# A graph network of four layers on one core: edge sources, destinations and weights stored as one table of rows

## The chip, the core and the metric

The kernel runs on one core of a Trainium2 chip. A core has five engines, each with its own instruction queue: TensorE (PE: matmuls, with PEld for the weight loads), VectorE (DVE), ScalarE (ACT), GpSimd (POOL) and SyncE (SP, which only issues DMAs). They share an on-chip memory of 128 partitions and 16 DMA engines that move data to and from device memory. The metric is the device time of one execution in microseconds (us). 0.2% of it, 13.2 us, is about what a measurement can tell from no change.

## The reference

There are 6250 nodes of 128 features and 100000 edges; `dst` is sorted, `src` is random. Each layer normalizes, applies a relu, passes messages along the edges, sums them by destination and adds the result to `x`:

```
edge_index = stack([src, dst])
x = x + L0(relu(layernorm(x)), edge_index, edge_weight)       # gather * weight, segment_sum, @W0, batch norm, relu
x = x + L1(relu(layernorm(x)), edge_index)                    # relu(h@Wmsg+b)[src], segment_sum, update, + h
x = x + L2(relu(layernorm(x)), edge_index, edge_attr_64)      # silu/sigmoid message from [h[src], h[dst], e]
x = x + L3(relu(layernorm(x)), node_vec1, src, dst, edge_attr_4, edge_attr_8)
```

In layer 0 `edge_index[0]` (src) is the row that is summed into and `edge_index[1]` (dst) the one gathered from, with the factor `edge_weight`.

## The kernel before

**Work items.** The sorted edges are cut into 782 rows of 128 (`ROWS`; 781 whole ones and one of 32 edges, filled up by 96). Nodes are in 49 blocks of 128, one partition for each node of a block. An item is one row of edges seen from one node block; there are 832 (`ITEMS`), and the setup finds for each its block and its row of edges. The item tables `src_it`, `rel_it` and `w_it` hold, for each item, the 128 sources, the 128 destinations relative to the block and the 128 weights, one item to a column.

**Setup, up to the first barrier.** ACT copies `src`, `dst` and `edge_weight` to device-memory arrays `e_src`, `e_dst`, `e_w` (L966), padded to a whole number of rows. SP loads `dst` for DVE (L349), then `x` (L354, L355), 34 weights and biases (L357), then stores what a possible sort would need: `blk_i`, `blk_f`, `bin_next` (L360 to L363). POOL writes the filling of the last row (L558, six DMAs), clears a buffer of zeros (L561), drains, stores it to four arrays `sums0` to `sums3` (L565), which layer 0 adds its messages to, and waits for the plan and for SP's three stores (`blocks_out`, L616). `dst` is sorted here, so the branch L573 to L612 is not run. Then POOL issues 21 indirect gathers (L625 to L627, for each of seven chunks of 128 items one from each of the three arrays): partition p gets the 512 bytes of its item's row. DVE meanwhile makes the plan (L1166 to L1221), then scales weights (L1256 to L1267), waits at L1273 until all 21 gathers have landed (`meta_rows`), turns what came into floats (L1275 to L1279), and PE transposes it into the item tables (L695, copies L1285). At the end of it each engine drains its queue and waits until all five have done so (`barrier`, L237): the first barrier, L628 on POOL, L1291 on DVE. Behind it DVE starts the layer norm (L1296); POOL waits for the zeroing (L632) and goes to a second barrier, which ends `node_tables(0)`.

**Layer 0.** For each item SP loads the row of sources to all partitions (`src_b`, L392), DVE, PE and ACT make a 128x128 tile of messages, and POOL adds it to one of the four `sums` by an indirect DMA (L642), 832 times. Layers 1 to 3 gather node rows with 2496 indirect DMAs (L670). The order on every engine is that of the program text; DMAs of different engines share the 16 DMA engines.

Of the kernel before, what the change touches and what calls it, by code (L numbers as in the profile page):

```python
# [18 lines left out]
ALU = mybir.AluOpType  # L19
ACT = mybir.ActivationFunctionType  # L20
F32 = mybir.dt.float32
I32 = mybir.dt.int32
# [3 lines left out]
P = 128  # L26
N = 6250
E = 100000
# [3 lines left out]
ROWS = (E + P - 1) // P  # L32
EPAD = ROWS * P
# [4 lines left out]
META = CHUNKS * P  # L38
# [19 lines left out]
def gnn_layers(nc, x, src, dst, edge_attr_4, edge_attr_64, edge_attr_8, edge_weight,  # L58
               W0, gamma, beta, Wmsg, bmsg, Wupd, bupd, w1, b1, w2, b2, wg, bg, wu, bu,
               wl1s, wl1v, fc1, fc2, wl2s, wl2v, out):  # L60
    with ExitStack() as ctx:
# [8 lines left out]
        def dram(name, shape, dt=F32):  # L70
            return nc.dram_tensor(name, shape, dt, kind="Internal").ap()


        e_src, e_dst, e_w = dram("e_src", [EPAD, 1], I32), dram("e_dst", [EPAD, 1], I32), dram("e_w", [EPAD, 1])
        e_a4, e_a8, e_a64 = dram("e_a4", [2 * EPAD, 4]), dram("e_a8", [2 * EPAD, 8]), dram("e_a64", [2 * EPAD, 64])
        e_pre = dram("e_pre", [QUADS + 4, P, 4, 256])
        blk_f, blk_i, bin_next = dram("blk_f", [E, 1]), dram("blk_i", [E, 1], I32), dram("bin_next", [64, 1])
# [206 lines left out]
        def landed(each, ring, q, k, lag):  # L284
# [2 lines left out]
                return each * ((q - lag) // ring + 1)  # L287
            return (q - k) * (each // ring) + each * ((k - lag) // ring + 1)

        def batches(layer):  # L290

            n = NODE_BATCH[layer]
            return [(i, b, min(n, NBT - b)) for i, b in enumerate(range(0, NBT, n))]
# [53 lines left out]
        def _(sp):  # L347
# [33 lines left out]
            def load_attributes(layer):  # L381

                ph = EDGE[layer]
                freed = ph["dup_done"]
                regs = [sp.alloc_register(f"row{layer}_{k}") for k in range(RING)]

                def top(turn):
                    sp.load(regs, row_row[0:1, bass.ds(turn + LEAD, RING)])

                def load(k, turn):  # L390
                    r = sp.snap(regs[k], min_val=0, max_val=ROWS - 1)
                    sp.dma_start(src_b[:, k, :], e_src[bass.ds(r * P, P), :].rearrange("e o -> (o e)").partition_broadcast(P)  # L392
                                 ).then_inc(attr_in[k], 16)

                half = sp.value_load(copy_to[0:1, 0:1], min_val=0, max_val=EPAD)

                def copy(at, n):
                    for to, of in ((e_a64, edge_attr_64), (e_a8, edge_attr_8), (e_a4, edge_attr_4)):
                        even = lambda a: a.rearrange("e k -> (e k)").rearrange("(q c) -> q c", q=16 if n == FIRST else P)
                        sp.dma_start(even(to[bass.ds(half + at, n), :]),  # L400
                                     even(of[bass.ds(at, n) if not isinstance(at, int) else slice(at, at + n), :])).then_inc(a64_copied, 16)

                top(0)
                for k in range(RING):
                    load(k, 0)
                copy(0, FIRST)
                with sp.Fori(RING, ITEMS - RING + 1, RING) as turn:
                    copy((turn - RING) * (PIECE // RING) + FIRST, PIECE)
                    top(turn)
                    for k in range(RING):  # L410

                        held(sp, freed, turn + (k - RING + 1))
                        load(k, turn)
# [107 lines left out]
        def _(pool):  # L521
# [31 lines left out]
            pool.wait_ge(tail_ready, 1)  # L553

            def tails():
                for to, of in ((e_src, s_i[0:TN, 0:1]), (e_dst, s_i[0:TN, 1:2]), (e_w, s_f[0:TN, 0:1]),
                               (e_a4, s_64[0:TN, 0:4]), (e_a8, s_64[0:TN, 0:8]), (e_a64, s_64[0:TN, 0:64])):
                    pool.dma_start(to[T0:EPAD, :], of).then_inc(tails_in, 16)  # L558
            tails()
            zeros = big[:, 9000:9000 + (NBT + 1) * P]  # L560
            g.memset(zeros, 0.0)  # L561
            pool.drain().then_inc(tail_ready, 1)
            pool.wait_ge(tail_ready, 2)
            for k in range(COPIES):
                pool.dma_start(sums[k].rearrange("(p b) d -> p (b d)", p=P), zeros).then_inc(scattered[k], 16)  # L565
            pool.wait_ge(tails_in, 6 * 16)


# [4 lines left out]
            with pool.Else():  # L573


                pool.wait_ge(blocks_out, 48)
                pool.wait_ge(small_copied, 48)

                def tile(t, e0, n, first):
                    sl = slice(e0, e0 + n) if isinstance(e0, int) else bass.ds(e0, n)  # L580
                    if not first:

                        held(pool, sort_pos, t)
                        for k in range(2):
                            held(pool, sort_out[k], t * 48)
                        held(pool, sort_bin, t * 16)
                    pool.dma_start(s_bb[:, 0:n], blk_f[sl, :].rearrange("e o -> o e").partition_broadcast(P)).then_inc(sort_in[0], 16)
                    for q, (to, of) in enumerate(((s_f[0:n, 1:2], blk_f[sl, :]), (s_i[0:n, 2:3], blk_i[sl, :]),
                                   (s_i[0:n, 0:1], src[sl].rearrange("(e o) -> e o", o=1)),
                                   (s_i[0:n, 1:2], dst[sl].rearrange("(e o) -> e o", o=1)),  # L590
                                   (s_f[0:n, 0:1], edge_weight[sl].rearrange("(e o) -> e o", o=1)),
                                   (a12[0:n, 0, 0:4], edge_attr_4[sl, :]), (a12[0:n, 1, 0:8], edge_attr_8[sl, :]),
                                   (s_64[0:n, :], edge_attr_64[sl, :]))):
                        pool.dma_start(to, of).then_inc(sort_in[q // 4], 16)
                    held(pool, sort_in[0], t * 80 + 80)
                    held(pool, sort_in[1], t * 64 + 64)
                    pool.indirect_dma_start(s_f[0:n, 2:3], None, bin_next,
                                            bass.IndirectOffsetOnAxis(ap=s_i[0:n, 2:3], axis=0)).then_inc(sort_base, 16)

                    held(pool, sort_rank, t + 1)  # L600
                    pool.dma_start(bin_next, s_f[0:64, 5:6]).then_inc(sort_bin, 16)
                    at = bass.IndirectOffsetOnAxis(ap=s_i[0:n, 3:4], axis=0)
                    for q, (to, of) in enumerate(((e_src, s_i[0:n, 0:1]), (e_dst, s_i[0:n, 1:2]), (e_w, s_f[0:n, 0:1]),
                                                  (e_a4, a12[0:n, 0, 0:4]), (e_a8, a12[0:n, 1, 0:8]), (e_a64, s_64[0:n, :]))):
                        pool.indirect_dma_start(to, at, of, None).then_inc(sort_out[q // 3], 16)
                full = E // P
                tile(0, 0, P, True)
                with pool.Fori(1, full) as t:
                    tile(t, t * P, P, False)
                tile(full, full * P, E - full * P, False)  # L610
                for k in range(2):
                    pool.wait_ge(sort_out[k], (full + 1) * 48)  # L612

            pool.nop()

            pool.wait_ge(blocks_out, 48)  # L616
            pool.wait_ge(small_copied, 48)


            rows128 = lambda a: a.rearrange("(r e) o -> r (e o)", e=P)  # L620
            m_i = big[:, 0:2 * META].bitcast(I32)
            m_w = big[:, 2 * META:3 * META]
            for c in range(CHUNKS):
                at = bass.IndirectOffsetOnAxis(ap=it_ai[:, c:c + 1], axis=0)
                pool.indirect_dma_start(m_i[:, c * P:(c + 1) * P], None, rows128(e_src), at).then_inc(meta_rows, 16)  # L625
                pool.indirect_dma_start(m_i[:, META + c * P:META + (c + 1) * P], None, rows128(e_dst), at).then_inc(meta_rows, 16)
                pool.indirect_dma_start(m_w[:, c * P:(c + 1) * P], None, rows128(e_w), at).then_inc(meta_rows, 16)  # L627
            barrier(pool)  # L628


# [330 lines left out]
        @block.scalar  # L961
        def _(act):
            a = nc.scalar
            flat = lambda a, c: a.rearrange("(q c) o -> q (c o)", c=c)
            for to, of in ((e_src, src), (e_dst, dst), (e_w, edge_weight)):
                act.dma_start(flat(to[0:E, :], EC), of.rearrange("(q c) -> q c", c=EC)).then_inc(small_copied, 16)  # L966

            act.wait_ge(const_ready, 3)
            act.wait_ge(blocks_ready, 1)
# [182 lines left out]
        def _(dve):  # L1152
# [114 lines left out]
            v.tensor_scalar(Wl2[32:64, 1, 0:32], Wl2[32:64, 1, 0:32], float(3 ** -0.5), None, ALU.mult)  # L1267


            m_i = big[:, 0:2 * META].bitcast(I32)  # L1270
            m_w = big[:, 2 * META:3 * META]
            m_f = big[:, 3 * META:6 * META]
            dve.wait_ge(meta_rows, 16 * 3 * CHUNKS)  # L1273
            link(v.tensor_scalar(it_off[:], it_b[:], float(P), None, ALU.mult))
            v.tensor_copy(m_f[:, 0:META], m_i[:, 0:META])  # L1275
            v.tensor_copy(m_f[:, 2 * META:3 * META], m_w)
            for c in range(CHUNKS):
                lo = META + c * P
                last = v.tensor_scalar(m_f[:, lo:lo + P], m_i[:, lo:lo + P], it_off[:, c:c + 1], None, ALU.subtract)  # L1279
            dve.drain().then_inc(meta_rel, 1)  # L1280
            for q in range(3 * CHUNKS):
                dve.wait_ge(meta_T, q + 2)
# [413 lines left out]
```

## Time and profile before

| | us |
|---|---|
| three runs | 6579.94, 6580.35, 6586.99 (median 6580.35) |
| profiled execution | 6581.73 |
| its span | 6580.1 |
| setup, to the first instruction behind the first barrier | 119.08 |
| layer 0's first indirect sum | 170.22 |
| POOL busy in the whole span | 3778.7 (57%) |
| PE, DVE, ACT busy | 4451.8, 3511.6, 1918.0 |

A profile shows one execution. In a timeline a row is an instruction or several like ones on one engine, with its start, its length, and in brackets how long the engine had been idle and what released it. SPq and ACTq are the queues that issue DMAs: the length is that of the issue, not of the transfer. In a table of windows stand the busy time of each engine in a stretch, the granted clock of TensorE as a share of its full clock, the mean busy share of the 16 DMA engines, and the GB/s that they moved.

### The profile page before, as it was taken

The numbers are of one execution on the slowest core, as the hardware profiler recorded it, in microseconds if no ns is written. First come the engines' busy times: TensorE is split into PE (matmuls) and PEld (weight loads), VectorE is DVE, ScalarE is ACT, GpSimd is POOL, SyncE is SP. The second block draws the span as 40 slices with busy tenths as digits, with TensorE's granted clock in tenths as the row PEclk, the third lists the DMA queues.
The fourth block names the chain that finished last, engine by engine and source line by source line (L and its number), as shares of the span: only waits on it lengthen the run. The fifth ranks groups of instructions, "written<-read, shape, count | busy, mean of one in ns | idle before, by whom it ended". The sixth has DMA issues, their size and how long they took to land. (4 is left out here: it accounts for less than half of the span.)

```text
span 6580.1 us, 113728 instructions
## 1 busy us (share of the span) xinstructions
PE 4451.8 (68%) x21582; PEld 3403.9 (52%) x21583; DVE 3511.6 (53%) x11197; ACT 1918.0 (29%) x5540; POOL 3778.7 (57%) x3395
## 2 busy tenths in 40 slices
PE   1888888888345555656777777777765666666667
PEld 1666666666234444444565656565554444444445
DVE  5655555555443232332655655555565555656555
ACT  2322222222122222222322222222243333333333
POOL 2888888888356666665255555555515454555443
PEclk9555555555577777777889888888886667777667
DMA  4666665666434454444244444444412222222222
GB/s 135 101 90 93 89 93 92 90 92 90 95 112 152 155 156 152 154 154 148 97 138 139 140 136 138 136 141 134 137 55 39 37 38 37 37 38 37 37 38 44
DMA packets 822279, 660.17 MB, mean 100 GB/s; under 512 B 444329, under 2 KB 711251, under 8 KB 820826
## 3 DMA queue, kind: packets, MB, share of 16 engines
q0 software_dynamic: 214432, 287.62, 22.0%
q1 hardware_dynamic: 607674, 370.53, 20.3%
q10 hardware_dynamic: 96, 1.20, 0.1%
q8 instruction: 24, 0.39, 0.0%
q14 instruction: 53, 0.43, 0.0%
HBM read 464.78 MB, written 225.68 MB: 105 GB/s over the span
## 5 line engine op out<-in xcount | busy, mean ns | idle before, releaser
L670 POOL DMA_INDIRECT G<-table,src_it x2496 | 2417.5, 969 | 2121.0 <-issue 651.1
L1388 DVE TENSOR_TENSOR big<-psum,big 128x129 f32 (+2 forms) x2496 | 823.6, 330 | 1225.0 <-remote 596.0
L642 POOL DMA_INDIRECT sums<-work,idx x832 | 1284.1, 1543 | 318.4 <-issue 179.2
L800 PE MATMUL psum<-work 128*128 128x128 f32 x1664 | 631.0, 482 | 192.8 <-DVE work L1435 115.0
L887 PE MATMUL psum<-big,oh 128*128 128x256 f32 x1664 | 643.7, 554 | 8.2 <-ACT big L1091 3.5
L1037 ACT ACTIVATE work<-psum,work 128x128 f32<-128x128 f32 x832 | 305.4, 367 | 1066.4 <-PE psum L792 667.4
L800 PEld LDWEIGHTS psum<-work 128*128 128x128 f32 x1664 | 414.0, 308 | 384.0 <-DVE work L1435 243.5
L747 PE MATMUL psum<-We,work 64*128 64x256 f32 x1664 | 347.0, 552 | 375.1 <-ACT work L1016 295.0
L1375 DVE TENSOR_TENSOR oh<-iota,rel_it 128x512 f32<-128x512 f32 x625 | 438.5, 702 | 298.5 <-remote 143.5
L792 PE MATMUL psum<-big,work 128*128 x1664 | 586.1, 455 | 0.0
L887 PEld LDWEIGHTS psum<-big,oh 128*128 128x128 f32 x1664 | 444.7, 280 | 134.0 <-issue 41.8
L1427 DVE TENSOR_SCALAR work<-G,src_it 128x128 f32<-128x128 int32 x832 | 268.3, 322 | 392.1 <-PE psum L800 308.6
L878 PE MATMUL psum<-ident,work 128*32 128x128 f32 x208 | 69.0, 332 | 557.3 <-DMA work<-e_a 431.6
L747 PEld LDWEIGHTS psum<-We,work 64*128 64x128 f32 x1664 | 212.9, 268 | 435.8 <-issue 352.5
L792 PEld LDWEIGHTS psum<-big,work 128*128 128x128 f32 x1664 | 414.2, 309 | 26.3 <-issue 8.7
L784 PE MATMUL psum<-ident,oh 128*128 128x128 f32 x832 | 366.3, 440 | 83.8 <-issue 46.9
L1050 ACT ACTIVATE work<-psum 128x512 f32<-128x512 f32 x208 | 124.2, 597 | 969.4 <-remote 512.2
L820 PE MATMUL psum<-big,work 128*128 x2496 | 377.0, 300 | 31.2 <-ACT work L1063 28.0
L1009 ACT ACTIVATE work<-psum 128x256 f32<-128x256 f32 x208 | 79.7, 383 | 970.0 <-remote 480.6
L1075 ACT ACTIVATE work<-psum 32x128 f32<-32x128 f32 x208 | 55.4, 266 | 1019.5 <-PE psum L878 676.4
L1493 DVE TENSOR_TENSOR work<-psum,work 128x512 f32<-128x512 f32 x416 | 267.2, 684 | 157.8 <-remote 72.9
L1435 DVE COPY work<-psum 128x128 f32<-128x128 f32 x832 | 242.5, 291 | 179.8 <-DMA sums<-work,idx 172.5
(230 smaller groups left out, 7709.9 us busy)
## 6 DMA issues: line engine op xcount, KB each, us to landing
e_pre<-work SPq DMA_DIRECT2D x208, 512.0 KB
work<-e_pre SPq DMA_DIRECT2D x208, 512.0 KB
G<-e_src SPq DMA_DIRECT2D x832, 64.0 KB
G<-table,src_it POOLq DMA_INDIRECT x2496
work<-e_a SPq DMA_DIRECT2D x832, 32.0 KB
e_a<-in_edge_attr_dram SPq DMA_DIRECT2D x51, 488.0 KB
sums<-work,idx POOLq DMA_INDIRECT x832
work<-e_a SPq DMA_DIRECT2D x832, 4.0 KB
```

The lines of the kernel that those rows point to most:

```text
L642: pool.indirect_dma_start(sums[k % COPIES], bass.IndirectOffsetOnAxis(ap=idx[:, k:k + 1], axis=0), z_out[:, k, :], None, compute_op=ALU.ad ...
L670: pool.indirect_dma_start(G[:, k, 0:wid], None, tab, bass.IndirectOffsetOnAxis(ap=src_it[:, n:n + 1], axis=0)).then_inc(quad_in[k // 4], 16)
L747: mm = t.matmul(bank[5 + j % 2][:, j // 2 * 256:j // 2 * 256 + 256], eT1[h:h + 64, (k - 1) % 2, j // 2, :], We2[h:h + 64, :], start=True, ...
L784: t.transpose(bank[s % 2][:, 0:P], oh[:, s, :], ident[:]).then_inc(ph["t_done"], 1)
L792: t.matmul(bank[2 + s % 2][:, 0:P], ohT[:, s % 4, :], at(Tz, b), start=True, stop=True).then_inc(ph["row_done"], 1)
L800: t.matmul(bank[4 + s % 2][:, 0:P], same[:, s % 4, :], scaled[:, s % 4, :], start=True, stop=True).then_inc(ph["sum_done"], 1)
L820: mm = t.matmul(bank[1 + j // 2][:, j % 2 * 256:j % 2 * 256 + 256], ohT2[:, j, :], Qp[:, bass.ds(b, 1), piece * 256:(piece + 1) * 256].rea ...
L887: mm = t.matmul(bank[4 + k % 2 * 2 + j // 2][:, j % 2 * 256:j % 2 * 256 + 256], oh[:, k % 4 * 4 + j, :], msg3[:, k % 4, j, :], start=True, ...
L1037: a.activation(scaled[:, s % 4, :], bank[2 + s % 2][:, 0:P], ACT.Copy, scale=w_it[:, bass.ds(n - 4, 1)]).then_inc(ph["w_done"], 1)
L1375: v.tensor_tensor(oh[:, k % 4 * 4:k % 4 * 4 + 4, :], iota[:].unsqueeze(1).broadcast_to([P, 4, P]), rel_it[:, bass.ds(q * 4, 4)].unsqueeze( ...
L1388: v.tensor_tensor(to, ps, to, ALU.add).then_inc(EDGE[layer]["acc_done"], 1)
L1427: v.tensor_scalar(same[:, s % 4, :], src_b[:, s, :], src_it[:, bass.ds(n - 1, 1)], None, ALU.is_equal).then_inc(ph["same_ready"], 1)
```

## The change

The three arrays become one table `e_meta` of 782 rows with 3 x 128 elements, so 1536 bytes: sources, destinations, weights of a row of edges side by side.

- ACT copies each input into its third of the rows (`meta_parts`: 781 pieces of 512 bytes and one short piece), six DMAs in place of three.
- POOL's three small tail stores go to the last row of `e_meta`.
- POOL zeroes `sums0` and `sums1` where it zeroed all four, and `sums2` and `sums3` behind the gathers, before the first barrier.
- The gathers are 7 of 1536 bytes a partition in place of 21 of 512 bytes. DVE reads the three parts with a stride, and waits for 7.
- Layer 0's loads of sources read the first third of a row of `e_meta`.
- If `dst` were not sorted, the sorted arrays would be copied into `e_meta` too; this isn't run.

```diff
@@ -71,7 +71,8 @@
             return nc.dram_tensor(name, shape, dt, kind="Internal").ap()
 
 
-        e_src, e_dst, e_w = dram("e_src", [EPAD, 1], I32), dram("e_dst", [EPAD, 1], I32), dram("e_w", [EPAD, 1])
+        e_src, e_dst, e_w = dram("e_src", [E, 1], I32), dram("e_dst", [E, 1], I32), dram("e_w", [E, 1])
+        e_meta = dram("e_meta", [ROWS, 3, P], I32)
         e_a4, e_a8, e_a64 = dram("e_a4", [2 * EPAD, 4]), dram("e_a8", [2 * EPAD, 8]), dram("e_a64", [2 * EPAD, 64])
         e_pre = dram("e_pre", [QUADS + 4, P, 4, 256])
         blk_f, blk_i, bin_next = dram("blk_f", [E, 1]), dram("blk_i", [E, 1], I32), dram("bin_next", [64, 1])
@@ -287,6 +288,14 @@
                 return each * ((q - lag) // ring + 1)
             return (q - k) * (each // ring) + each * ((k - lag) // ring + 1)
 
+        def meta_parts(src, dst, weight):
+
+            whole = ROWS - 1
+            for q, of in enumerate((src, dst, weight)):
+                to = e_meta.bitcast(F32) if q == 2 else e_meta
+                yield to[0:whole, q, :], of[0:whole * P].rearrange("(r e) -> r e", e=P)
+                yield to[whole:ROWS, q, 0:E - whole * P], of[whole * P:E].rearrange("(r e) -> r e", r=1)
+
         def batches(layer):
 
             n = NODE_BATCH[layer]
@@ -389,7 +398,7 @@
 
                 def load(k, turn):
                     r = sp.snap(regs[k], min_val=0, max_val=ROWS - 1)
-                    sp.dma_start(src_b[:, k, :], e_src[bass.ds(r * P, P), :].rearrange("e o -> (o e)").partition_broadcast(P)
+                    sp.dma_start(src_b[:, k, :], e_meta[bass.ds(r, 1), 0, :].rearrange("o e -> (o e)").partition_broadcast(P)
                                  ).then_inc(attr_in[k], 16)
 
                 half = sp.value_load(copy_to[0:1, 0:1], min_val=0, max_val=EPAD)
@@ -553,16 +562,21 @@
             pool.wait_ge(tail_ready, 1)
 
             def tails():
-                for to, of in ((e_src, s_i[0:TN, 0:1]), (e_dst, s_i[0:TN, 1:2]), (e_w, s_f[0:TN, 0:1]),
-                               (e_a4, s_64[0:TN, 0:4]), (e_a8, s_64[0:TN, 0:8]), (e_a64, s_64[0:TN, 0:64])):
+                for q, of in enumerate((s_i[0:TN, 0:1], s_i[0:TN, 1:2], s_f[0:TN, 0:1])):
+                    to = e_meta.bitcast(F32) if q == 2 else e_meta
+                    pool.dma_start(to[ROWS - 1, q, P - TN:P].rearrange("(e o) -> e o", o=1), of).then_inc(tails_in, 16)
+                for to, of in ((e_a4, s_64[0:TN, 0:4]), (e_a8, s_64[0:TN, 0:8]), (e_a64, s_64[0:TN, 0:64])):
                     pool.dma_start(to[T0:EPAD, :], of).then_inc(tails_in, 16)
             tails()
             zeros = big[:, 9000:9000 + (NBT + 1) * P]
             g.memset(zeros, 0.0)
             pool.drain().then_inc(tail_ready, 1)
             pool.wait_ge(tail_ready, 2)
-            for k in range(COPIES):
+
+            def zero(k):
                 pool.dma_start(sums[k].rearrange("(p b) d -> p (b d)", p=P), zeros).then_inc(scattered[k], 16)
+            for k in range(2):
+                zero(k)
             pool.wait_ge(tails_in, 6 * 16)
 
 
@@ -574,7 +588,7 @@
 
 
                 pool.wait_ge(blocks_out, 48)
-                pool.wait_ge(small_copied, 48)
+                pool.wait_ge(small_copied, 96)
 
                 def tile(t, e0, n, first):
                     sl = slice(e0, e0 + n) if isinstance(e0, int) else bass.ds(e0, n)
@@ -610,21 +624,24 @@
                 tile(full, full * P, E - full * P, False)
                 for k in range(2):
                     pool.wait_ge(sort_out[k], (full + 1) * 48)
+                column = lambda a: a.rearrange("e o -> (e o)")
+                for to, of in meta_parts(column(e_src), column(e_dst), column(e_w)):
+                    pool.dma_start(to, of).then_inc(sort_in[0], 16)
+                pool.wait_ge(sort_in[0], (full + 1) * 80 + 96)
 
             pool.nop()
 
             pool.wait_ge(blocks_out, 48)
-            pool.wait_ge(small_copied, 48)
-
-
-            rows128 = lambda a: a.rearrange("(r e) o -> r (e o)", e=P)
-            m_i = big[:, 0:2 * META].bitcast(I32)
-            m_w = big[:, 2 * META:3 * META]
+            pool.wait_ge(small_copied, 96)
+
+
+            meta_rows_of = e_meta.rearrange("r t e -> r (t e)")
+            m_all = big[:, 0:3 * META].bitcast(I32)
             for c in range(CHUNKS):
-                at = bass.IndirectOffsetOnAxis(ap=it_ai[:, c:c + 1], axis=0)
-                pool.indirect_dma_start(m_i[:, c * P:(c + 1) * P], None, rows128(e_src), at).then_inc(meta_rows, 16)
-                pool.indirect_dma_start(m_i[:, META + c * P:META + (c + 1) * P], None, rows128(e_dst), at).then_inc(meta_rows, 16)
-                pool.indirect_dma_start(m_w[:, c * P:(c + 1) * P], None, rows128(e_w), at).then_inc(meta_rows, 16)
+                at_rows = bass.IndirectOffsetOnAxis(ap=it_ai[:, c:c + 1], axis=0)
+                pool.indirect_dma_start(m_all[:, c * 3 * P:(c + 1) * 3 * P], None, meta_rows_of, at_rows).then_inc(meta_rows, 16)
+            for k in range(2, COPIES):
+                zero(k)
             barrier(pool)
 
 
@@ -961,9 +978,8 @@
         @block.scalar
         def _(act):
             a = nc.scalar
-            flat = lambda a, c: a.rearrange("(q c) o -> q (c o)", c=c)
-            for to, of in ((e_src, src), (e_dst, dst), (e_w, edge_weight)):
-                act.dma_start(flat(to[0:E, :], EC), of.rearrange("(q c) -> q c", c=EC)).then_inc(small_copied, 16)
+            for to, of in meta_parts(src, dst, edge_weight):
+                act.dma_start(to, of).then_inc(small_copied, 16)
 
             act.wait_ge(const_ready, 3)
             act.wait_ge(blocks_ready, 1)
@@ -1267,16 +1283,17 @@
             v.tensor_scalar(Wl2[32:64, 1, 0:32], Wl2[32:64, 1, 0:32], float(3 ** -0.5), None, ALU.mult)
 
 
-            m_i = big[:, 0:2 * META].bitcast(I32)
-            m_w = big[:, 2 * META:3 * META]
+            m_i = big[:, 0:3 * META].bitcast(I32).rearrange("p (c t e) -> p c t e", t=3, e=P)
+            m_w = big[:, 0:3 * META].rearrange("p (c t e) -> p c t e", t=3, e=P)
+            chunked = lambda a: a.rearrange("p (c e) -> p c e", e=P)
             m_f = big[:, 3 * META:6 * META]
-            dve.wait_ge(meta_rows, 16 * 3 * CHUNKS)
+            dve.wait_ge(meta_rows, 16 * CHUNKS)
             link(v.tensor_scalar(it_off[:], it_b[:], float(P), None, ALU.mult))
-            v.tensor_copy(m_f[:, 0:META], m_i[:, 0:META])
-            v.tensor_copy(m_f[:, 2 * META:3 * META], m_w)
+            v.tensor_copy(chunked(m_f[:, 0:META]), m_i[:, :, 0, :])
+            v.tensor_copy(chunked(m_f[:, 2 * META:3 * META]), m_w[:, :, 2, :])
             for c in range(CHUNKS):
                 lo = META + c * P
-                last = v.tensor_scalar(m_f[:, lo:lo + P], m_i[:, lo:lo + P], it_off[:, c:c + 1], None, ALU.subtract)
+                last = v.tensor_scalar(m_f[:, lo:lo + P], m_i[:, c, 1, :], it_off[:, c:c + 1], None, ALU.subtract)
             dve.drain().then_inc(meta_rel, 1)
             for q in range(3 * CHUNKS):
                 dve.wait_ge(meta_T, q + 2)
```

On POOL, from the end of the unused sort branch to layer 0. `big` is the on-chip buffer that the gathered rows go to. Before:

```order
L625 DMA big<-e_src,big 128x128 [waits small_copied,blocks_out]
L626 DMA big<-e_dst,big 128x128
L627 DMA big<-e_w,big 128x128
...
L627 DMA big<-e_w,big 128x128
L644 UNCONDITIONAL_BRANCH [waits scattered2,scattered1,scattered3,scattered0,phase_end]
L644 ISA
```

The same place in the changed program (L577 is the zeroing):

```order
L642 DMA big<-e_meta,big 128x384 [waits small_copied,blocks_out]
L642 DMA big<-e_meta,big 128x384 x6
L577 DMA sums<-big 128x6528 x2
L661 UNCONDITIONAL_BRANCH [waits scattered2,scattered1,scattered3,scattered0,phase_end]
L661 ISA
```

21 gathers have become 7, and two zeroings stand between them and the barriers. Earlier on POOL, from the last tail stores on, before:

```order
L558 DMA e_a<-big 96x8
L558 DMA e_a<-big 96x64
L561 MEMSET big 128x6528
L565 DMA sums<-big 128x6528 [waits tail_ready]
L565 DMA sums<-big 128x6528 x3
L570 TENSOR_LOAD big [waits plan_ready,tails_in]
```

and now:

```order
L569 DMA e_a<-big 96x8
L569 DMA e_a<-big 96x64
L572 MEMSET big 128x6528
L577 DMA sums<-big 128x6528 [waits tail_ready]
L577 DMA sums<-big 128x6528
L584 TENSOR_LOAD big [waits plan_ready,tails_in]
```

Two zeroings are left there of four. The start of ACT's queue, before:

```order
L966 DMA e_src<-in_src_dram 16x6250
L966 DMA e_dst<-in_dst_dram 16x6250
L966 DMA e_w<-in_edge_weight_dram 16x6250
L974 ACT_TABLE_LOAD [waits blocks_ready]
L974 ACTIVATE big<-big 125x800 [waits const_ready]
```

and now:

```order
L982 DMA e_meta<-in_src_dram 781x128
L982 DMA e_meta<-in_src_dram 16x2
L982 DMA e_meta<-in_dst_dram 781x128
L982 DMA e_meta<-in_dst_dram 16x2
L982 DMA e_meta<-in_edge_weight_dram 781x128
L982 DMA e_meta<-in_edge_weight_dram 16x2
L990 ACT_TABLE_LOAD [waits blocks_ready]
```

Three copies of 16 pieces of 25000 bytes have become three of 781 pieces of 512 bytes, with a short one behind each.

## Rows read from the trace of the kernel before

**Rows 1.** DVE timeline in the setup: start, us, engine, line, what [idle before, releaser].

```profile
9.71 5.30 DVE L1166 TENSOR_SCALAR big<-big 125x800 int32<-125x800 int32 x1 [9.59 <-DMA big<-in_dst_dram]
...
51.22 0.20 DVE L1219 TENSOR_REDUCE s_f<-big 64x1 f32<-64x50 f32 x1
...
107.16 0.17 DVE L1274 TENSOR_SCALAR big<-big 128x7 f32<-128x7 f32 x1 [32.33 <-DMA big<-e_w,big]
...
119.08 9.77 DVE L1296 BATCH_NORM_STATS2 bn_raw<-X 128x6 f32<-128x128 f32 x50
```

**Rows 2.** POOL timeline, setup and start of layer 0.

```profile
9.00 5.57 POOL L561 MEMSET big<- 128x6528 f32 x1
21.81 2.17 POOL L565 DMA_DIRECT2D sums<-big  x4 [7.24 <-POOLq L562]
78.86 1.03 POOL L625 DMA_INDIRECT big<-e_src,big  x1 [54.87 <-DMA bin_next<-s_f]
...
104.09 0.95 POOL L627 DMA_INDIRECT big<-e_w,big  x1 [0.30 <-issue]
170.22 1.61 POOL L642 DMA_INDIRECT sums<-work,idx  x1 [65.19 <-DVE work L1435]
```

**Rows 3.** Timeline of SP's DMA queue in the setup.

```profile
5.29 16.68 SPq L355 DMA_DIRECT2D X<-in_x_dram  x1
22.01 1.83 SPq L357 DMA_DIRECT2D big<-in_L_gnn_W_dram  x1
...
37.46 2.01 SPq L357 DMA_DIRECT2D w2s<-in_L_gnn_w_dram  x1
39.51 14.29 SPq L357 DMA_DIRECT2D wus<-in_L_gnn_wu_dram  x2
53.84 1.45 SPq L357 DMA_DIRECT2D big<-in_L_gnn_b_msg_dram  x1
...
60.33 6.10 SPq L357 DMA_DIRECT2D Wl<-in_L_gnn_w_lin_v_dram  x9
66.47 0.55 SPq L360 DMA_DIRECT2D blk_i<-big  x1
...
67.45 0.51 SPq L363 DMA_DIRECT2D bin_next<-s_f  x1
```

**Rows 4.** Windows of the setup; last two columns DMA share and GB/s.

```profile
10.00:20.00 10.00, 0.00 (x0) 0.00 (x0) 9.66 (x14) 3.73 (x6) 4.58 (x1) 1.00 1.07 147
40.00:50.00 10.00, 0.64 (x2) 0.50 (x2) 8.44 (x26) 0.00 (x0) 0.00 (x0) 1.00 1.02 437
66.00:79.00 13.00, 0.90 (x3) 0.50 (x3) 5.25 (x12) 0.00 (x0) 0.14 (x1) 1.00 0.29 63
110.00:120.00 10.00, 5.91 (x35) 5.07 (x35) 7.60 (x30) 0.00 (x0) 0.00 (x0) 1.00 0.00 0
```

**Rows 5.** DMA issues of the setup: KB each, us from issue to landing.

```profile
e_w<-in_edge_weight_dram ACTq DMA_DIRECT2D x1, 390.6 KB, 7.0
...
e_a<-big POOLq DMA_DIRECT2D x1, 24.0 KB, 12.5
```

**Rows 6.** Waits in the setup: us in total, times, longest.

```profile
ACT L974 <- DVEq L1171: 16.3, 1, 16.3
```

**Rows 7.** POOL's drain of line 562: duration ns min/median/max, start.

```profile
L562 POOLq DRAIN  x1: 13557/13557/13557, 7.7 to 7.7; - x1
```

**Rows 8.** POOL's drain at the first barrier.

```profile
L237 POOLq DRAIN  x1: 18216/18216/18216, 90.0 to 90.0; - x1
```

**Rows 9.** POOL's drain behind its last tensor operation of layer 0.

```profile
L237 POOLq DRAIN  x1: 4179/4179/4179, 1812.9 to 1812.9; - x1
```

**Rows 10.** That operation in the timeline.

```profile
1812.95 4.07 POOL L654 TENSOR_TENSOR big<-big,work 128x1280 f32<-128x1280 f32 x1 [1.43 <-DVE big L1649]
```

**Rows 11.** Layer 2's gathers of 1024 bytes a row.

```profile
L670 POOL DMA_INDIRECT G<-table,src_it x678: 940/946/1944, 3224.2 to 4499.4; - x170
```

**Rows 12.** What POOL's 832 indirect sums of layer 0 waited for.

```profile
  issue: 179.2, 588
```

## The prediction

> **What bounds the kernel now.** I read the page first, to see how much of the span the change can touch, then each engine's timeline of the setup, and last the waits and drains that release the next stage. Layer 0's loop is POOL's: of its 832 indirect sums 588 waited only the 0.30 us that any issue takes (179.2 us in all) [rows 12], and the loop's other parts don't change in kind. The change sits in the setup, so that is where time can come from. Every engine meets at the first barrier; DVE passes it at 119.08 us [rows 1], and all that follows is in a row behind it.
>
> Going back from 119.08: DVE got its gathered rows at 107.16, after 32.33 us of doing nothing [rows 1], and needed 11.92 us from there to the barrier. POOL issued the first of the 21 gathers at 78.86 and the last at 104.09 for 0.95 us, one each 1.26 us [rows 2]. So the gathers are bound by POOL's issue, not by bytes: the last one was there 2.1 us after its issue ended. POOL could not start before 78.86 because it waited for SP's store of `bin_next`, after 54.87 us idle [rows 2]. SP issued that store only at 67.45 [rows 3].
>
> Why so late? SP's queue shows two stalls. L355 held it for 16.68 us, until 21.97, while the rows of `x` were moved. Then, as the four zeroings ran, the loads of `wus` held it for 14.29 us, where its neighbours take 1.3 to 2.0 us each [rows 3]. In this stretch the DMA engines are full, share 1.02 at 437 GB/s [rows 4]. One zeroing of 3264 KB takes 7.65 us at that rate, four 30.6 us; from 21.81 on [rows 2] that ends near 53, and SP moves again at 53.84. The weights wait behind zeros that nobody needs before 170.22, the first indirect sum [rows 2].
>
> The plan itself is ready early: DVE's last step of it starts at 51.22 [rows 1].
>
> **The change part by part.**
>
> *Two zeroings less in front.* Two end 15.3 us after they start, near 38, so at 39.5, when SP comes to `wus`, the DMA engines are free. Two such loads cost about 2.6 us then in place of 14.29: SP gains 11.7 us. Behind it the 12.6 us from 53.84 to 66.47, small loads and nine of single elements (6.10 us), stay [rows 3], and so do the 11.4 us from `bin_next`'s issue to POOL's start. If the weights had some other stall, this term would be 0; more than 14.3 us it cannot give.
>
> *The copies into rows.* 781 pieces of 512 bytes three times over are 2343 pieces. The nearest row is the load of `x`, 6144 pieces of 512 bytes: 16.7 us of stall [rows 3], 2.7 ns a piece, in a window at 147 GB/s with the engines full [rows 4]. By that the copies take 6.4 us of DMA time. The old ones, 1.2 MB in large pieces, took at least 2.7 us at 437 GB/s. They stand in front of `x`, so `x`, the tail stores and with them the drain and SP's release come later by 3.7 us. From below the term is 0 (hidden in gaps of the first 10 us: the old copies landed within 7.0 us of their issue [rows 5]); from above, with all pieces at twice the pace of `x`, it is 10. I take 4. That ACT has to issue six DMAs costs nothing: it waits until 16.3 us for DVE [rows 6]. DVE's own start, which waits for `dst` until 9.71, is covered too: its first instruction took 5.30 us instead of well under 1, until POOL's clearing ended at 14.57 [rows 1, 2], so a delay of 4 us is hidden there, and SP comes to `bin_next` 8 us behind the plan even when sped up.
>
> What the pieces do to the 16 engines is where a rule of the notes speaks against the change. The two stores of `blk_i` and `blk_f` have 125 pieces each and ran at a DMA share of 0.29 and 63 GB/s [rows 4]. By the Trainium skill (DMA: Bandwidth & Descriptors, section "Why a DMA increments its semaphore by 16 and not by 1") a DMA runs on the largest number of engines up to 16 that divides its outer dimension; for 125 that is 5, and 5/16 agrees with the share. By the same rule 781 gives 11 engines, the copies would take 6.4 x 16/11 = 9.3 us on these, and the term would be 6.6 in place of 4, an estimate; the sum below would be 2.6 us less.
>
> So POOL's first gather starts at 78.86 - 11.7 + 4 = 71.2.
>
> *7 gathers for 21.* A gather's issue doesn't depend on the bytes of a row: 946 ns at 1024 bytes [rows 11], 950 at 512 [rows 2]. 1536 bytes are not in the trace. I take the same; from above, if it grew by the share of bytes, 1.4 us each, that would be 3 us more in all. 196 KB each 1.26 us are 156 GB/s, well under 437. The seven end 6 x 1.26 + 0.95 = 8.5 us behind the first, at 79.7, and DVE has them at 81.8. The casts read the same number of elements in runs of 128: unchanged. DVE would be at the barrier at 93.7.
>
> *Two zeroings behind.* Here the cost comes back. They are issued at 80.0, take 15.3 us at 437 GB/s on engines that are otherwise idle (0 GB/s from 110 to 120 [rows 4]) and land about 2.1 us later, at 97.4. Nothing reads them before layer 0, and the scatter's own waits come at the second barrier. But POOL has to drain before the first barrier, and its drain appears to wait for its DMAs. The drain of L562 began at 7.7 and took 13.56 us, to 21.26 [rows 7], though the clearing in front of it had ended at 14.57 [rows 2]; the last tail store, issued by 9.0, took 12.5 us to land, so till about 21 [rows 5]. At the first barrier it ended at 90.0 + 18.22 = 108.2 [rows 8], 1.0 us after the gathers had landed and 3.2 after POOL's last issue. With no DMA of POOL's in front it ends within 0.1 us of the operation: 1812.9 + 4.18 against 1812.95 + 4.07 [rows 9, 10]. With a drain 1.0 behind the landing POOL arrives at 98.4, 4.7 us later than DVE, and the barrier opens at about 98.6.
>
> *Layer 0's loads* from `e_meta` are as long as before, 512 bytes to each partition, and the loop is POOL's. The fewer instructions in the setup change nothing else.
>
> **Sum.** 98.6 against 119.08: 20.5 us less. The profiled execution took 6581.7, which gives 6561.2; the runs' median is 1.4 below it, so 6560. Where the barrier opens is the only thing that counts: 27.4 us behind the first gather in place of 40.2 (12.8 us), and the first gather 7.7 earlier.
>
> **The rivals.**
>
> A2: the drain doesn't wait for data, only for POOL's own descriptor work. For it: a drain could end later for other reasons, and all three examples also fit a slow end of that work. Then DVE sets the barrier at 93.7: 25.4 us less, 6555.
>
> B: SP's stall isn't the zeroing's. Its queue may simply be full of pieces of the weights, which move slowly in any company. Then the first gather starts at 78.9 to 82.9, and the barrier gains 12.8 less up to 4, so 6568 to 6572. Against it: the stall ends when the zeros must end.
>
> C, the slower side: the copies into rows clog the start. They write and read device memory in small pieces, which no row shows. At six times the piece of `x`, 16 ns, they take 38 us, 35 more than before, and everything behind `x` (tails, drain, zeroing, weights) moves by that in place of 4: 35 - 24.5 = 10.5 us slower, 6591; at seven times it would be over 0.2%. It turns slower from 11.6 ns a piece. Against it: nothing in the trace makes a 512 byte piece cost over 3.5 ns.
>
> That the table brings nothing because the gathers' bytes bind is excluded by 156 GB/s. I give little to the rest of the run shifting: runs of one kernel lie within 7 us.
>
> **How the numbers follow.** The forecast (barrier at the end of the second zeroings) 0.52, A2 0.20, B 0.19, C 0.05, some other 0.04. The forecast's own range with the copies at 0 to 10 us and the gathers up to 3 slower is 6556 to 6569; A2 goes down to 6551; B up to 6572. The range over all is 6550 to 6575. 13.2 us, 0.2% of the time, is about what a measurement can tell from no change. Faster by more holds for A2, nearly all of the forecast and a little of B: 0.71. Within it: most of B and the rest, 0.23. Slower: C and some rest, 0.06.
>
> **What would show it.** SP's two loads of `wus` take under 4 us together; if they still take 14, B. POOL's first gather at 69 to 74; seven gathers 1.26 apart. DVE's wait for them ends near 82. Behind it the windows show some 430 GB/s for 15 us, and POOL's drain ends behind these; if DVE goes on at 94 with zeros still moving, A2. The load of `x` releasing SP at 26 instead of 22 gives the copies' cost; at over 40 it is C. What would make the prediction wrong in another way is a change behind the barrier: layer 0's sums must still stand 0.30 us apart, and the stretch from the barrier to the end must be 6461 us long.

## Result and the profile after

| | before | after |
|---|---|---|
| median of 14 runs each, us | 6584.41 (6565.63 to 6593.7) | 6566.36 (6555.51 to 6581.39) |
| ratio, 95% interval | | 0.9976 (0.9967 to 0.9986) |
| profiled execution, its span | 6581.73, 6580.1 | 6571.13, 6569.5 |
| setup, to the first instruction behind the first barrier | 119.08 | 97.82 |

The ratio is 15.8 us less, with an interval of 9.2 to 21.7: faster. (The two medians lie 18.1 us apart, in the same interval.) The 20.5 forecast lie in it too, so the time alone doesn't tell whether some of them are missing. The setup itself gained 21.3 us. In the lines that answer to [rows 2], POOL's timeline of the changed kernel shows two zeroings in front, seven gathers and two zeroings behind:

```profile
22.00 1.12 POOL L577 DMA_DIRECT2D sums<-big  x2 [7.23 <-POOLq L573]
70.31 1.04 POOL L642 DMA_INDIRECT big<-e_meta,big  x1 [47.19 <-DMA bin_next<-s_f]
...
77.97 0.95 POOL L642 DMA_INDIRECT big<-e_meta,big  x1 [0.30 <-issue]
78.92 1.16 POOL L577 DMA_DIRECT2D sums<-big  x2
149.16 1.63 POOL L659 DMA_INDIRECT sums<-work,idx  x1 [69.08 <-DVE work L1452]
```

The first gather starts 8.6 us earlier than before, its bracket still names `bin_next`; an issue takes 0.95 us with 1536 bytes a row as it did with 512. DVE's timeline [rows 1] has the rows 11.6 us behind the first gather where it was 28.3:

```profile
7.52 0.58 DVE L1182 TENSOR_SCALAR big<-big 125x800 int32<-125x800 int32 x1 [7.40 <-DMA big<-in_dst_dram]
...
8.45 6.75 DVE L1185 CAST big<-big 125x800 f32<-125x800 int32 x1
...
81.87 0.17 DVE L1291 TENSOR_SCALAR big<-big 128x7 f32<-128x7 f32 x1 [15.67 <-DMA big<-e_meta,big]
82.07 1.09 DVE L1292 CAST big<-big 128x896 f32<-128x896 int32 x1
83.08 1.07 DVE L1293 COPY big<-big 128x896 f32<-128x896 f32 x1
...
97.82 9.76 DVE L1313 BATCH_NORM_STATS2 bn_raw<-X 128x6 f32<-128x128 f32 x50 [3.22 <-SPq L238]
```

The last row is new: DVE stood idle for 3.22 us in front of the first barrier. It names SP, whose last issue of the setup was at 65.8; the engine that came last is POOL. Its two drains answer to [rows 7] and [rows 8]: the one behind the tail stores, and the one at the first barrier (min/median/max in ns, first and last start in us).

```profile
L573 POOLq DRAIN  x1: 13717/13717/13717, 7.7 to 7.7; - x1
```

```profile
L238 POOLq DRAIN  x1: 27704/27704/27704, 70.1 to 70.1; - x1
```

The second ends at 70.1 + 27.7 = 97.8. The windows [rows 4] show what still moved until then, the zeros at 431 GB/s (DMA share and GB/s last):

```profile
80.00:90.00 10.00, 4.33 (x21) 4.09 (x21) 7.50 (x29) 0.00 (x0) 0.09 (x1) 1.00 1.01 431
90.00:100.00 10.00, 1.69 (x14) 1.09 (x14) 5.00 (x20) 0.00 (x0) 0.00 (x0) 0.81 0.59 254
100.00:110.00 10.00, 0.00 (x0) 0.00 (x0) 8.66 (x46) 1.16 (x1) 0.00 (x0) 0.50 0.00 0
```

SP's queue [rows 3] shows where the time in front went:

```profile
5.29 18.39 SPq L364 DMA_DIRECT2D X<-in_x_dram  x1
23.73 1.44 SPq L366 DMA_DIRECT2D big<-in_L_gnn_W_dram  x1
25.21 1.47 SPq L366 DMA_DIRECT2D big<-in_L_gnn_W_msg_dram  x1
26.72 7.25 SPq L366 DMA_DIRECT2D big<-in_L_gnn_W_upd_dram  x1
34.01 5.99 SPq L366 DMA_DIRECT2D WPQ<-in_L_gnn_w_dram  x1
40.04 1.10 SPq L366 DMA_DIRECT2D WPQ<-in_L_gnn_wg_dram  x1
...
46.52 0.91 SPq L366 DMA_DIRECT2D wus<-in_L_gnn_wu_dram  x2
...
57.74 0.55 SPq L369 DMA_DIRECT2D blk_i<-big  x1
...
58.73 0.51 SPq L372 DMA_DIRECT2D bin_next<-s_f  x1
```

The stall at `wus` is gone (0.91 us for two in place of 14.29), but two other loads stall in front of it, for 7.25 and 5.99 us. `blk_i` is issued at 57.74 in place of 66.47. Last, layer 0's indirect sums, 832 of them: min, median and max in ns.

```profile
L659 POOL DMA_INDIRECT sums<-work,idx x832: 1537/1545/1678, 149.2 to 1690.0; - x167
```

The median is 5 ns more than before, where it was 1540.

### The profile page after: what moved, and what is told of

Read it like the earlier page. It is cut to its first block and busy times, and to the rows that moved or that the text cites. A ratio compares the mean times of both kernels' runs of the same rounds, so it can differ in the third digit from the quotient of the medians.

```text
span 6569.5 us, 113717 instructions
## 1 busy us (share of the span) xinstructions
PE 4416.8 (67%) x21582; PEld 3377.5 (51%) x21583; DVE 3517.6 (54%) x11197; ACT 1918.4 (29%) x5540; POOL 3771.0 (57%) x3381
```

## Experiments

**The two kernels again.** Each was profiled a second time, unchanged.

> The kernel before, profiled again. Theory S (the stages behind the first barrier vary by themselves between executions): setup ends at 119.1 again within 0.3 us, layer 0 from the barrier to the clearing for layer 1 is 1703.5 us within some us, and layers 2 and 3 (1739.5 and 1654.9 us in the first profile) differ from these by up to 15 us. Theory L (layer 0's loop is slower in the changed kernel because of it): layer 0 repeats 1703.5 within 1 us and a sum takes 1540 ns.

> The changed kernel, profiled again. Theory S: setup ends at 97.8 to 98.0, and its layers 2 and 3 (1753.8 and 1644.1 us in the first profile) come out otherwise by up to 15 us; layer 0's 1709.5 too. Theory L: layer 0 again takes 1709.5 us within 1 us and a sum 1545 ns, where before they were 1703.5 and 1540.

The stages, cut at the first instruction behind the first barrier and at POOL's clearing for each next layer (us; layer 3 here runs to the end of the span, which the expectations cut off):

| | setup | layer 0 | layer 1 | layer 2 | layer 3 | span |
|---|---|---|---|---|---|---|
| before | 119.1 | 1703.5 | 1324.0 | 1740.0 | 1693.6 | 6580.1 |
| before, again | 118.8 | 1704.4 | 1323.7 | 1750.2 | 1690.0 | 6587.1 |
| after | 97.8 | 1709.7 | 1324.9 | 1754.2 | 1682.9 | 6569.5 |
| after, again | 97.4 | 1708.9 | 1322.6 | 1755.1 | 1669.3 | 6553.3 |

The setup repeats within 0.4 us. Layer 2 of the kernel before differed by 10 us between its two profiles, layer 3 of the changed one by 14. So both theories hold in part. The first pair of profiles lost 14.2 us in layer 2 and won 10.7 in layer 3, where nothing was changed. But layer 0 is 4.5 to 6.2 us longer in both executions of the changed kernel, while it repeats within 1 us. In the second profile of each the median indirect sum is again 1540 and 1545 ns:

```profile
L642 POOL DMA_INDIRECT sums<-work,idx x832: 1532/1540/1675, 170.3 to 1706.8; - x167
```

```profile
L659 POOL DMA_INDIRECT sums<-work,idx x832: 1537/1545/1662, 149.6 to 1690.0; - x167
```

SP's queue in the second profile of the kernel before spreads its stall otherwise:

```profile
36.24 4.21 SPq L357 DMA_DIRECT2D We<-in_L_gnn_wg_dram  x1
40.49 1.37 SPq L357 DMA_DIRECT2D w2s<-in_L_gnn_w_dram  x1
41.91 11.31 SPq L357 DMA_DIRECT2D wus<-in_L_gnn_wu_dram  x2
...
66.17 0.70 SPq L360 DMA_DIRECT2D blk_i<-big  x1
```

`wus` takes 11.31 us in place of 14.29, and yet `blk_i` is issued within 0.3 us of the first profile's 66.47. Which load is held differs from run to run. The end of the queue hardly does: `blk_i` is issued at 66.2 to 66.8 in the three profiles that have this front.

**The gathers alone.** All four zeroings stay in front:

```diff
-            for k in range(2):
+            for k in range(COPIES):
                 zero(k)
             pool.wait_ge(tails_in, 6 * 16)
...
-            for k in range(2, COPIES):
-                zero(k)
             barrier(pool)
```

> The table of rows and the 7 gathers, but all four zeroings in front. Theory: POOL's first gather starts at 79 to 82, as the weights stay behind four zeroings; the last ends 8.6 us later, DVE has the rows near 91, the first barrier opens at 104 with DVE last (it needs 12.7 us from there), POOL's drain is over by 94. About 15 us less than before. Rival (the parts need each other: the copies cost what the gathers save): over 110.

Ratio 0.9988 (0.9977 to 0.9999). POOL's and DVE's timelines:

```profile
84.11 1.04 POOL L642 DMA_INDIRECT big<-e_meta,big  x1 [60.16 <-DMA bin_next<-s_f]
```

```profile
107.80 9.76 DVE L1311 BATCH_NORM_STATS2 bn_raw<-X 128x6 f32<-128x128 f32 x50
```

Setup 11.3 us shorter, not 15: the first gather is 5.3 us later than before, where 0 to 3 was expected. The copies into rows cost more than the forecast said. The ratio (0.6 to 15.1 us less) fits the setup. Here `wus` isn't held at all though four zeroings stand in front: its two loads took 0.91 us. Four loads in front of them were held for 5.6 to 8.1 us each, and `blk_i` came at 71.73.

**The zeroings alone.** Three arrays, 21 gathers; only the order of the zeroings is new:

```diff
-            for k in range(COPIES):
+            def zero(k):
                 pool.dma_start(sums[k]..., zeros).then_inc(scattered[k], 16)
+            for k in range(2):
+                zero(k)
...
+            for k in range(2, COPIES):
+                zero(k)
             barrier(pool)
```

> The three arrays and 21 gathers of before, with two zeroings in front and two behind the gathers. Theory (the drain waits for the second zeroings): first gather at 67 to 69, last one's issue ends near 94, zeros landed near 112, POOL last at the barrier, which opens at 112 to 113: only 6 to 7 us less than before, though the gathers start 10 earlier. Rival (the drain doesn't matter): DVE goes on at 96 + 12 = 108, 11 us less.

Ratio 1.0001 (0.9987 to 1.0015). SP's queue, POOL, DVE, and last POOL's drain at the first barrier:

```profile
37.94 2.58 SPq L357 DMA_DIRECT2D wus<-in_L_gnn_wu_dram  x2
40.56 0.29 SPq L357 DMA_DIRECT2D big<-in_L_gnn_b_msg_dram  x1
...
50.78 0.55 SPq L360 DMA_DIRECT2D blk_i<-big  x1
```

```profile
63.81 1.04 POOL L627 DMA_INDIRECT big<-e_src,big  x1 [40.66 <-DMA bin_next<-s_f]
```

```profile
108.88 9.76 DVE L1300 BATCH_NORM_STATS2 bn_raw<-X 128x6 f32<-128x128 f32 x50 [5.15 <-SPq L237]
```

```profile
L237 POOLq DRAIN  x1: 31383/31383/31383, 77.5 to 77.5; - x1
```

The first gather starts at 63.8, 15.1 us earlier, but the setup is only 10.2 shorter: 21 gathers end late, and DVE then waits 5.15 us for POOL's drain, which ends at 77.5 + 31.4 = 108.9. That the drain sets the barrier was expected, the time was not: the barrier was put at 112 to 113 and came at 108.9, as the first gather came 3 to 5 us before the 67 to 69 expected. The two loads of `wus` take 2.58 us, as the prediction had put them (2.6).

**Zeroings behind the barrier.** The changed kernel with two lines in another order:

```diff
+            barrier(pool)
             for k in range(2, COPIES):
                 zero(k)
-            barrier(pool)
```

> As the changed kernel, but the last two zeroings are issued behind the first barrier. Theory (the drain waits for them): POOL's drain ends near 81, DVE is last, and the barrier opens 12.7 us behind its rows, at 94.6 in place of 97.8; the zeros run until about 113, before the second barrier, so the 3.2 us stay won. Rival (something else than the zeroings keeps POOL's drain): barrier at 97 to 98 again. The indirect sums take 1540 or 1545 ns: no theory yet.

Ratio 0.9969 (0.9958 to 0.998). POOL's drain and DVE's first instruction behind the barrier:

```profile
L238 POOLq DRAIN  x1: 11442/11442/11442, 69.3 to 69.3; - x1
```

```profile
93.17 9.76 DVE L1313 BATCH_NORM_STATS2 bn_raw<-X 128x6 f32<-128x128 f32 x50
```

The drain ends at 69.3 + 11.4 = 80.7 in place of 97.8, and the barrier opens 4.65 us earlier. Of this 3.2 are DVE's wait, which is gone, and 0.7 the landing of the rows. The last 0.75 are an earlier first gather, and that says nothing of the edit: this kernel, the changed one and two further below (the swap and the eighth gather) do the same work up to the gathers, and their five profiles have the first gather anywhere from 69.6 to 70.5. The first indirect sum comes at 146.0 in place of 149.2 and 149.6, so most of the gain is still there. (From the barrier to that sum the thirteen profiles took 51.1 to 52.9 us, so 1.5 us in this stretch can't be read.) The rival is out.

**One zeroing in front, three behind the barrier.**

```diff
-            for k in range(2):
-                zero(k)
+            zero(0)
             pool.wait_ge(tails_in, 6 * 16)
...
-            for k in range(2, COPIES):
-                zero(k)
             barrier(pool)
+            for k in range(1, COPIES):
+                zero(k)
```

> One zeroing in front, three behind the first barrier. Theory (each zeroing in front holds SP's weights for its own 7.65 us): first gather 7.65 earlier than the changed kernel's 70.3, at 62.7; DVE has its rows at 74, barrier at 87, 11 us earlier than the changed kernel; zeros end near 113, still before the second barrier (near 122). Rival (DVE's plan, ready at 51, or SP's own issue is the bound by then): first gather at 66 or later, barrier at 90 or later.

Ratio 0.995 (0.9933 to 0.9967).

```profile
64.24 1.05 POOL L641 DMA_INDIRECT big<-e_meta,big  x1 [40.93 <-DMA bin_next<-s_f]
```

```profile
87.85 9.76 DVE L1312 BATCH_NORM_STATS2 bn_raw<-X 128x6 f32<-128x128 f32 x50
```

First gather 6.1 us earlier, not 7.65, barrier 10.0 us earlier, not 11: near the theory, 1.6 and 1.0 short of it. One zeroing in front held the queue for less than its own length.

**The copies in 768 pieces and 13.** The counts of the waits for the copies go up with it.

```diff
-                yield to[0:whole, q, :], of[0:whole * P].rearrange("(r e) -> r e", e=P)
+                even = whole // 16 * 16
+                yield to[0:even, q, :], of[0:even * P].rearrange("(r e) -> r e", e=P)
+                yield to[even:whole, q, :], of[even * P:whole * P].rearrange("(r e) -> r e", e=P)
```

> As the changed kernel, but each copy into rows is cut into 768 pieces and 13 pieces. Theory (781 pieces go to 11 of the 16 engines, and so hold the load of x longer): the copies land earlier, and the first gather comes 1 to 3 us before 70.3. Rival (the pieces' number counts, not how they are spread): 70.3 within 0.5, or later for the three more DMAs.

```profile
5.29 17.42 SPq L366 DMA_DIRECT2D X<-in_x_dram  x1
22.76 1.62 SPq L368 DMA_DIRECT2D big<-in_L_gnn_W_dram  x1
...
25.66 1.23 SPq L368 DMA_DIRECT2D big<-in_L_gnn_W_upd_dram  x1
26.93 1.22 SPq L368 DMA_DIRECT2D WPQ<-in_L_gnn_w_dram  x1
...
52.44 0.55 SPq L371 DMA_DIRECT2D blk_i<-big  x1
```

```profile
64.68 1.04 POOL L644 DMA_INDIRECT big<-e_meta,big  x1 [41.09 <-DMA bin_next<-s_f]
```

```profile
91.76 9.76 DVE L1315 BATCH_NORM_STATS2 bn_raw<-X 128x6 f32<-128x128 f32 x50 [3.30 <-SPq L238]
```

The same bytes in the same pieces, cut otherwise, and three DMAs more: the first gather comes 5.6 us earlier, where 1 to 3 was expected, and is only 0.9 behind that of the kernel without any copies into rows (63.8). The two stalls of 7.25 and 5.99 us are gone. So most of the copies' cost was the way they were cut, and the 0.9 that is left is no more than the first gather of an unchanged front varies (69.6 to 70.5, above). This is one profile of each. No view here shows which of the 16 engines took the pieces, so that they were few with 781 is inferred.

**One tiny plain store, a swap, an eighth gather.** Three tests of the 5 ns of each indirect sum, one profile each. The first adds, behind the 21 gathers of the kernel before, a 64 byte store, which POOL waits for behind the barrier:

```diff
+            pool.dma_start(scratch, s_f[0:16, 0:1]).then_inc(tails_in, 16)
             barrier(pool)
```

> The kernel before with one tiny plain store (16 x 4 bytes, result unused) behind POOL's gathers. Theory D (what the last plain DMA before the loop leaves behind slows each indirect sum by 5 ns): a sum takes 1545 ns, as in the two kernels with zeroings behind the gathers. Rival (it needs the large zeroings, or their late landing): 1540 ns.

```profile
L645 POOL DMA_INDIRECT sums<-work,idx x832: 1535/1542/1661, 170.4 to 1707.8; - x167
```

The second zeroes `sums2` and `sums3` in front, the others behind:

```diff
-            for k in range(2):
+            for k in range(2, COPIES):
                 zero(k)
...
-            for k in range(2, COPIES):
+            for k in range(2):
                 zero(k)
```

> The changed kernel with sums2 and sums3 zeroed in front and sums0 and sums1 behind the gathers. Theory N (how many zeroings stand in front decides the 5 ns of each indirect sum): 1545 ns again. Rival (which of the arrays or semaphores came last decides): 1540 ns. Setup as in the changed kernel, 97.4 to 97.9.

```profile
L659 POOL DMA_INDIRECT sums<-work,idx x832: 1538/1546/1666, 149.6 to 1690.5; - x167
```

The third puts one more gather behind the zeroings, also waited for behind the barrier:

```diff
+            pool.indirect_dma_start(big[:, 15528:15912].bitcast(I32), None, meta_rows_of,
+                                    bass.IndirectOffsetOnAxis(ap=it_ai[:, 0:1], axis=0)).then_inc(tails_in, 16)
             barrier(pool)
```

> The changed kernel with an eighth gather (its result unused) behind the last zeroings. Theory D2 (the loop is slower where the last DMA before it was a plain one): 1540 ns a sum. Rival: 1545 ns, so the 5 ns come from something else that the order leaves. The drain must end about 2 to 4 us later than 97.7, as one more DMA stands in front of it.

```profile
L662 POOL DMA_INDIRECT sums<-work,idx x832: 1537/1545/1665, 149.5 to 1689.8; - x167
```

A small plain DMA at the end gives 1542, not 1545; a gather at the end leaves 1545; which arrays come last doesn't matter. The drain ended at 98.0, later than 97.8 but not by the 2 to 4 us expected. What goes with the number is the zeroings in front: the seven profiles with two have 1545 or 1546, the four with four 1540 to 1542, the two with one 1540 and 1541. Layer 0, from the barrier to POOL's clearing, goes with it: 1707.8 to 1710.7 us in the seven, 1703.5 to 1706.2 in the other six. With the zeroings all in front (the gathers alone) the table leaves it at 1540 ns and 1704.4 us, so neither comes from the table. Why is open.

**Both together.** 768 + 13 pieces, one zeroing in front and three behind the barrier; the edits are those of the two kernels above.

> Copies cut into 768 and 13 pieces, one zeroing in front, three behind the first barrier. Theory (the terms add until DVE's plan, ready at 51, is the bound): SP comes to its stores at 45, issues bin_next at 51, first gather at 58 to 60, barrier at 81 to 83, 36 to 38 us earlier than before; a sum takes 1541 ns. Time 0.994 to 0.995 of before. Rival (the waits behind the weights don't shrink any more): first gather at 64 again, as in each of the two alone.

Ratio 0.9943 (0.9922 to 0.9965), the lowest, though its interval overlaps that of one zeroing in front (0.9933 to 0.9967).

```profile
47.02 0.55 SPq L371 DMA_DIRECT2D blk_i<-big  x1
...
50.75 0.51 SPq L374 DMA_DIRECT2D bin_next<-s_f  x1
```

```profile
60.65 1.05 POOL L643 DMA_INDIRECT big<-e_meta,big  x1 [38.43 <-DMA bin_next<-s_f]
```

```profile
84.29 9.76 DVE L1314 BATCH_NORM_STATS2 bn_raw<-X 128x6 f32<-128x128 f32 x50
```

SP issues `bin_next` at 50.75, right as DVE's plan is ready (its last step ended at 50.7), though `blk_i` was issued at 47.02: the plan is the bound now. The first gather was expected at 58 to 60 and the setup 36 to 38 us shorter; it came at 60.65 and is 34.8 shorter.

## Why the prediction was right, and where it was off

**The mechanism held.** Two zeroings less let SP's weights through, seven gathers took 0.95 us each at 1536 bytes, DVE had the rows at 81.87 (forecast 81.8), and POOL's drain, waiting for zeros, set the barrier: 97.82 (forecast 98.6). A2 is out by the kernel with the zeroings behind the barrier, whose drain ends 17 us earlier. B is out by that with the zeroings alone, whose first gather came 15.1 us earlier. C is out: the changed kernel's `x` released SP at 23.7, not over 40.

**The two terms in front were each too small, and the errors cancelled.** That the first gather came at 70.3, for 71.2 forecast, is luck in this part. The zeroings' term was put at 11.7 us, from the stall at `wus` alone, and at 14.3 at most. In the kernel with the zeroings alone the two loads did take 2.58 us for 14.29, but `blk_i` came 15.7 us earlier (66.47 to 50.78) and the first gather 15.1: the small loads behind `wus` took 10.2 us in place of 12.6, and `wus` itself was reached 1.6 earlier. What the zeroings hold up is the queue, and not one row of it. Two zeroings are 15.3 us at 437 GB/s; they gave 15.1 without the copies into rows and 13.8 with them (84.1 to 70.3), both above the 11.7. (By the prediction's own figures four zeroings end at 52.4 and two at 37.1, where it says near 53 and near 38; nothing hangs on that.)

The copies were put at 4 us, and cost 6.5 with two zeroings in front (63.8 to 70.3) and 5.3 with four (78.9 to 84.1). The sign that the prediction named for this cost, SP's release by `x`, misses most of it: it came at 23.7 in place of 22.0, and the rest lay in the two loads that stalled behind.

The Trainium skill (DMA: Bandwidth & Descriptors, section "Why a DMA increments its semaphore by 16 and not by 1") takes the number of engines of a DMA from its outer dimension. The estimate by this rule, 6.6 us, was nearer than the 4 that I took from the mean pace of `x`. The kernel with 768 pieces agrees with the rule in that the cut matters. But the estimate's parts were wrong: in it the number of pieces costs 3.7 us (6.4 less 2.7) and the fewer engines 2.9 (9.3 less 6.4), where the runs show 0.9 and 5.6. That its total fitted is luck as well.

**One cost more, hidden.** DVE's two casts of strided parts took 1.09 and 1.07 us where they had taken 0.63 and 0.62, so DVE reached the barrier at 94.6 and not 93.7. The drain covered it. I had called them unchanged.

**What the sum left out.** "The fewer instructions in the setup change nothing else" failed: 832 sums at 5 ns more each are 4 us, and layer 0 is 4.5 to 6.2 us longer. 21.3 less some 5 is 16, near the timed 15.8, but the interval of 9.2 to 21.7 holds the 21.3 as well. The other ratios fit the same sum. For the zeroings alone the setup's 10.2 less 5 are within the interval of 1.0001 (8.5 us faster to 9.9 slower), and the 10.2 by themselves are not. Both together, 34.8 us without the 5 ns, is 0.9947 against 0.9943. The sign that the stretch behind the barrier must be 6461 us long could not be used: it was 6461.0 and 6468.3 in the two profiles before and 6471.7 and 6455.9 after.

**The spread** was underrated. I took 7 us from three runs; 14 runs of each kernel spread over 26 to 28 us. Whether the gain is above the 13.2 us that the prediction took as its line isn't settled either, as the interval starts at 9.2. In the four profiles layers 2 and 3 differ the most, so a single profile's span shows a gain of this size only when it is cut into stages.

## What to carry to other kernels

A large transfer that is issued early and needed late can delay small loads queued on another engine's queue by nearly its whole length: here two zeroings of 15.3 us delayed SP's queue by 13.8 to 15.1, one by 6.1 of 7.65. Issued late on POOL it was waited for by POOL's next drain, so here it belongs behind the barrier and not just in front of it. Read such a stall from the end of the queue, as the load that shows it differs from run to run. Before a copy is cut into rows, try a number of rows that divides evenly: here the cut of 781 into 768 and 13 gave back 5.6 of 6.5 us. And when two terms pull apart, test each alone: here both were wrong and the sum was right.

## What was not expected of the hardware

- POOL's indirect sums take 1545 or 1546 ns in all seven profiles with two zeroings in front and 1540 to 1542 in the six with four or one; neither the kind of the last DMA nor the array explains it. All seven also have exactly two zeroings behind the gathers, so which of the two counts isn't told apart.
- DVE's cast of 128x896 elements took 0.63 us from contiguous rows and 1.09 from parts of 128 in every 384.
- DVE's instruction of 800 elements that ran beside POOL's clearing of a buffer ended just behind it. Before, the shift (L1166) took 5.30 us from 9.71 to 15.0, and POOL's clearing ended at 14.6. After, `dst` came at 7.52, the shift was done before the clearing began and took 0.58, and the cast behind it took 6.75, until 15.2, with the clearing until 14.8. No run here moved the clearing away, so that it is the cause is not shown.
